# Cross-attention on one core: for two of four head groups GpSimd adds the two key halves of the probabilities, and the product with ones runs later on half as much

## What is computed

```python
def _L0_xattn_ref(q, v, k, Wq, bq, Wk, bk, Wv, bv, Wo, bo):
    NH = 16                       # heads of DK = 32
    qh = (q @ Wq.T + bq).reshape(b, s, NH, DK).transpose(0, 2, 1, 3)
    kh = (k @ Wk.T + bk).reshape(b, s, NH, DK).transpose(0, 2, 1, 3)
    vh = (v @ Wv.T + bv).reshape(b, s, NH, DK).transpose(0, 2, 1, 3)
    scores = einsum('bhqd,bhkd->bhqk', qh, kh) / sqrt(DK)
    probs = softmax(scores, axis=-1)
    ctx = einsum('bhqk,bhkd->bhqd', probs, vh)
    concat = ctx.transpose(0, 2, 1, 3).reshape(b, s, h)
    return concat @ Wo.T + bo
x = x + _L0_xattn_ref(_layernorm(x), ctx_1024, ctx_1024, ...)
```

## Time and profile before

| | us |
|---|---|
| median of 3 runs | 2575.8 (2575.73 to 2578.67) |
| the profiled execution, its own time | 2579.87 |
| its span in the profile | 2578.2 |
| TensorE (PE) busy | 2422.9 (94% of the span) |
| VectorE (DVE) busy | 1488.4 (58%) |
| ScalarE (ACT) busy | 1217.0 (47%) |
| GpSimd (POOL) busy | 651.0 (25%) |

### The profile page before, as it was taken

One profiled execution on the slowest core, in us unless ns is written; L12 is line 12 of the kernel. 1 busy time (PEld: TensorE's weight loads), 2 busy tenths in 40 slices (PEclk: granted clock), 3 DMA queues, 4 the chain that ended last, 5 costly groups with the idle time before them and its releaser, 6 DMA issues. The chain is left out here.

```text
span 2578.2 us, 47997 instructions
## 1 busy us (share of the span) xinstructions
PE 2422.9 (94%) x16982; PEld 2137.2 (83%) x16983; DVE 1488.4 (58%) x2585; ACT 1217.0 (47%) x1954; POOL 651.0 (25%) x1040
## 2 busy tenths in 40 slices
PE   7999999999997899999999983699999999999997
PEld 6999999999986788888888863488888888888896
DVE  6788888878873566666666655633343343334322
ACT  6655656656552444444444432334444353434342
POOL 3211111112114435454444511113030221303021
PEclk8999999999998899999999986799999999999999
DMA  4111111111126565656666522234152434424221
GB/s 133 39 40 50 39 38 56 35 44 48 39 65 179 146 199 154 191 165 187 177 180 184 157 86 86 65 110 108 67 133 75 110 82 126 103 73 113 89 59 20
DMA packets 237633, 261.01 MB, mean 101 GB/s; under 512 B 71112, under 2 KB 161224, under 8 KB 237360
## 3 DMA queue, kind: packets, MB, share of 16 engines
q1 hardware_dynamic: 196400, 237.48, 31.1%
q0 software_dynamic: 40960, 20.41, 4.5%
HBM read 182.47 MB, written 68.80 MB: 97 GB/s over the span
## 5 line engine op out<-in xcount | busy, mean ns | idle before, releaser
L2340 DVE TENSOR_TENSOR d_h_l<-d_hf,d_h_h 128x616 fp32r<-128x616 f32 x124 | 99.2, 800 | 391.0 <-ACT d_h_h L2137 391.0
L2037 PE MATMUL d_psH<-d_xgT_h,d_w_l 128*128 128x308 f32 x1024 | 314.7, 307 | 3.5 <-ACT d_hf L2189 2.1
L2189 ACT ACTIVATE d_hf<-d_psH,d_b1c 128x308 f32<-128x308 f32 x256 | 130.8, 518 | 385.8 <-PE d_psH L2039 385.8
L2038 PE MATMUL d_psH<-d_xgT_l,d_w_h 128*128 128x308 f32 x1024 | 311.5, 304 | 0.0
L2039 PE MATMUL d_psH<-d_xgT_h,d_w_h 128*128 128x308 f32 x1024 | 311.3, 304 | 0.0
L439 PE MATMUL a_psP<-s_xnT_h,s_w_l 128*128 128x256 f32 x1024 | 297.3, 290 | 5.8 <-ACT a_zs L691 2.7
L440 PE MATMUL a_psP<-s_xnT_l,s_w_h 128*128 128x256 f32 x1024 | 290.8, 284 | 0.0
L441 PE MATMUL a_psP<-s_xnT_h,s_w_h 128*128 128x256 f32 x1024 | 290.3, 284 | 0.0
L1999 POOL DMA_INDIRECT out_dram<-d_ob,d_to x40 | 103.7, 2592 | 686.0 <-ACT d_ob L2206 676.0
L2037 PE MATMUL d_psO<-d_w_h,d_h_l 128*123 128x512 f32 x620 | 244.2, 394 | 0.0
L2038 PE MATMUL d_psO<-d_w_l,d_h_h 128*123 128x512 f32 x620 | 244.0, 394 | 0.0
(11 more groups left out here) (399 smaller groups left out, 6103.0 us busy)
## 6 DMA issues: line engine op xcount, KB each, us to landing
d_w<-in_W_dram SPq DMA_DIRECT2D x64, 1024.0 KB, 6.4
b_qst<-qs_d SPq DMA_DIRECT2D x48, 512.0 KB, 6.7
b_kst<-ks_d SPq DMA_DIRECT2D x96, 256.0 KB, 4.0
s_raw<-in_x_dram SPq DMA_DIRECT2D x16, 512.0 KB, 3.6
s_xres<-in_x_dram SPq DMA_DIRECT2D x16, 512.0 KB, 3.6
x_d<-s_xres SPq DMA_DIRECT2D x16, 512.0 KB, 2.8
s_raw<-in_ctxT_dram SPq DMA_DIRECT2D x16, 512.0 KB, 9.6
s_xres<-x_d SPq DMA_DIRECT2D x16, 512.0 KB, 6.8
```

The source lines that it names most:

```text
L2037: pe.matmul(out, lo_w, hi_x, start=first, stop=False)
L2038: pe.matmul(out, hi_w, lo_x, start=False, stop=False)
L2189: act.activation(hf[:, m % 2, n * HALF:(n + 1) * HALF], psH[n][:, 0:HALF], ACT.Silu, bias=b1c[par][:, m:m + 1]).then_inc(silu_s, 1)
L2340: dve.tensor_tensor(out, a, b_, ALU.subtract).then_inc(done, 1)
```

## The change

For the groups j = 0 and 1 (`ADDED = 2`), `pv` does the product with V alone and raises a new semaphore `vp_mm`. GpSimd then adds the second key half of `PT` onto the first, in place (`pt_sum(j)`, one addition of 128 x 1024), and raises `pt_s`. TensorE does the product with ones later, on the added half alone (`sums(hb, j)`, 4 matmuls in place of 8, 8 instructions in place of 16): for group 0 behind turned(1,1), one K tile later, for group 1 behind K tile 7. `pv_mm` is now raised by `sums` for these two groups. Groups 2 and 3 stay as they are. In GpSimd's program pt_sum(0) stands between qk_parts(4) and max_parts(4), and pt_sum(1) between qk_parts(6) and max_parts(6); the `rsqrt` of sequence b-2 moves from behind max_parts(4) to ahead of pt_sum(0). ScalarE does exps(1,1) ahead of ctx_hi of group 0. VectorE does ctx_f of group 0 behind the third layer norm's `normalize` and row_max(2,1), and row_max(3,0) ahead of ctx_lo of group 0. In `experts_phase` two semaphores are merged into a third (`th_mm` and `mm_s` into `gr_mm`), with the waits raised to match; no instruction is added or moved there.

```diff
--- before.py
+++ after.py
@@ -1002,6 +1002,7 @@
         v_mm, v_cp = sem("v_mm"), sem("v_cp")
         s_mm, mx_s, mp_s, mt_mm, mr_s = (sem(n) for n in ("s_mm", "mx_s", "mp_s", "mt_mm", "mr_s"))
         st_mm, exp_s, pv_mm, cf_s, co_hi, co_lo = (sem(n) for n in ("st_mm", "exp_s", "pv_mm", "cf_s", "co_hi", "co_lo"))
+        vp_mm, pt_s = sem("vp_mm"), sem("pt_s")
         o_mm, x2_s, xb_s = sem("o_mm"), sem("x2_s"), sem("xb_s")
         r_tp, r_cp, r_mm, lg_s = sem("r_tp"), sem("r_cp"), sem("r_mm"), sem("lg_s")
 
@@ -1057,6 +1058,8 @@
         def second(b):
             return isinstance(b, int) and b == 1
 
+
+        ADDED = 2
         block = ctx.enter_context(nc.Block())
 
         @block.sync
@@ -1188,9 +1191,18 @@
                     g.tensor_tensor(mxp[:, j % 2, qt, KR + G:KX], mx[:, qt, :], f32(mxp[:, j % 2, qt, KR:KR + G]),
                                     ALU.subtract).then_inc(mp_s, 1)
 
+                def pt_sum(j):
+                    pool.wait_ge(vp_mm, ADDED * (b - 1) + j + 1)
+                    pool.sem_inc(passed_p, 1)
+                    g.tensor_tensor(PT[:, j % 2, :, 0, :], PT[:, j % 2, :, 0, :], PT[:, j % 2, :, 1, :], ALU.add).then_inc(pt_s, 1)
+
                 for i in range(U):
                     if cur:
                         qk_parts(i)
+                    if prev2 and i == 4:
+                        rsqrt(b - 2, ln3, ve3, rs3, rstd3)
+                    if prev and i in (4, 6):
+                        pt_sum(i // 2 - 2)
                     if prev:
                         max_parts(i)
                     if cur and i < KD and not first(b):
@@ -1204,8 +1216,6 @@
                             pool.wait_ge(p_ld, 96)
                         for t in range(TT):
                             g.tensor_tensor(xres[:, t, :], xres[:, t, :], bob[:], ALU.add).then_inc(xb_s, 1)
-                    if prev2 and i == 4:
-                        rsqrt(b - 2, ln3, ve3, rs3, rstd3)
                 if cur and not last(b) and not first(b):
                     rsqrt(b, ln, ve, rs, rstd)
                 if first(b):
@@ -1332,13 +1342,20 @@
                         wait(pe, x2_s, 2 * (b - 1))
                     if j == 2 and prev2:
                         pe.wait_ge(lg_s, b - 1)
-                    for half_, w in enumerate((V[v], None)):
+                    for half_, w in enumerate((V[v], None)[:1 if j < ADDED else 2]):
                         for kt in range(TT):
                             for h in range(G):
                                 c = slice((G * j + h) * DK, (G * j + h + 1) * DK)
                                 mm = pe.matmul(psV[h * DK:(h + 1) * DK, half_ * S:(half_ + 1) * S],
                                                ones[:] if w is None else w[:, kt, c], PT[:, j % 2, h, kt, :],
                                                start=kt == 0, stop=kt == TT - 1)
+                    mm.then_inc(vp_mm if j < ADDED else pv_mm, 1)
+
+                def sums(hb, j):
+
+                    pe.wait_ge(pt_s, ADDED * hb + j + 1)
+                    for h in range(G):
+                        mm = pe.matmul(psV[h * DK:(h + 1) * DK, S:2 * S], ones[:], PT[:, j % 2, h, 0, :], start=True, stop=True)
                     mm.then_inc(pv_mm, 1)
 
                 def out_proj(t):
@@ -1416,6 +1433,7 @@
                 if prev:
                     scores(2, 1)
                     turned(1, 1)
+                    sums(b - 1, 0)
 
                 if cur:
                     qk_tile(6)
@@ -1429,6 +1447,7 @@
                 if cur:
                     qk_tile(7)
                 if prev:
+                    sums(b - 1, 1)
                     turned(2, 0)
                     scores(3, 1)
 
@@ -1549,8 +1568,8 @@
                 if cur:
                     q_f(5)
                 if prev:
+                    exps(1, 1)
                     ctx_hi(b - 1, 0)
-                    exps(1, 1)
                 if prev2:
                     act.wait_ge(r_tp, b - 1)
                     copy(xn3T, psT[:], r_cp)
@@ -1674,15 +1693,15 @@
                         weights_lo(c)
                 if prev:
                     row_max(2, 0)
-                    ctx_f(b - 1, 0)
                 if prev2:
 
                     wait(dve, xn3_st, 16 * (b - 2))
                     normalize(b - 2, ln3, xres, mv3, rs3, rstd3, xn3)
                 if prev:
                     row_max(2, 1)
+                    ctx_f(b - 1, 0)
+                    row_max(3, 0)
                     ctx_lo(b - 1, 0)
-                    row_max(3, 0)
                 if more:
                     dve.wait_ge(xa_ld, 16 * b + 16)
                     for t in range(TT):
```

More of the change, by code:

```diff
@@ L1868, in experts_phase @@
         cn_s, th_s = csem("cn"), csem("th")
-        pre_s, mm_s = csem("pre"), csem("mm")
+        pre_s = csem("pre")
         key_s, cand_s, sign_s = csem("key"), csem("cand"), csem("sign")
-        gate_s, gt_mm, gr_mm, th_mm = csem("gate"), csem("gt_mm"), csem("gr_mm"), csem("th_mm")
+        gate_s, gt_mm, gr_mm = csem("gate"), csem("gt_mm"), csem("gr_mm")
         MADE = 12
@@ L2026, in _ @@
             pe.wait_ge(th_s, 1)
-            pe.matmul(psC, ones[:], digits[:].rearrange("p a e -> p (a e)"), start=True, stop=True).then_inc(th_mm, 1)
+            pe.matmul(psC, ones[:], digits[:].rearrange("p a e -> p (a e)"), start=True, stop=True).then_inc(gr_mm, 1)
             pe.wait_ge(made, MADE + 4)
@@ L2033, in _ @@
             pe.matmul(psA, ones_b[:], upto[:], start=False, stop=True)
-            pe.matmul(psC[:, 0:NE], ones_b[:], upto[:, 0, :, T - 1], start=True, stop=True).then_inc(mm_s, 1)
+            pe.matmul(psC[:, 0:NE], ones_b[:], upto[:, 0, :, T - 1], start=True, stop=True).then_inc(gr_mm, 1)
             def split_mm(out, hi_w, lo_w, hi_x, lo_x, first, last_):
@@ L2311, in _ @@
             dve.sem_inc(th_s, 1)
-            dve.wait_ge(th_mm, 1)
+            dve.wait_ge(gr_mm, ROUNDS + 1)
             did(dve.tensor_copy(hi_i[:], psC[:, 0:NE]))
@@ L2323, in _ @@
                                    both[:].rearrange("p a e t -> p (a e t)"), 0.0, ALU.mult, ALU.add).then_inc(pre_s, 1)
-            dve.wait_ge(mm_s, 1)
+            dve.wait_ge(gr_mm, ROUNDS + 2)
             did(dve.tensor_copy(cnt[:], psC[:, 0:NE]))
```

## The result

The changed kernel takes 2639.02 us (median of 4 runs, 2636.91 to 2644.08) against 2577.24 us of the kernel before on the same chip (2575.73 to 2580.93): a ratio of 1.0241, interval 1.0228 to 1.0254. It is 62 us slower; forecast were 50 us more and 2626 us. The profiled execution of it took 2639.2 us, its span is 2637.6 us.

A forecast was written before the change was run, and what follows sets the result against it. TensorE's program was taken as the bounding chain in attention, busy 392 of 400 us. Race 40, rest 2 and clock 8 gave 50 us on 2579.9, so 2630, or 2626 us for the median; range 2606 to 2644.

The forecast's parts named there:

- the race: After tile 6's take, TensorE needs one K tile, GpSimd split plus addition: 2.85 us in each of 14 bodies, 40 us.
- the clock in the full bodies: TensorE's clock drops behind new waits of 2.1 us: 6 of 14 bodies at 1.3 us, 8 us.
- The addition's price: GpSimd's addition of 128 x 1024, extrapolated from smaller two-input instructions: 2.36 us, bounds 2.0 to 3.1.
- The 0.28 us for contention: Extra time given to pt_sum(0) on GpSimd because VectorE's normalize runs beside it.
- Group 0: TensorE waits 0.9 us at sums(0), K tile 6 starts 0.75 us late, and this is absorbed before K tile 7.
- With 0.7 us of cover: ctx_f of group 0 ends at 1172.5, before pv of group 1 needs it at 1173.2, so costs nothing.
- K tile 7 starts at 1174.87 as before: Tile 6 is taken at 1174.34 as before, by store or copy; gains and losses ahead of it sum to 0.
- The rest: Body 1 1 us, body 15 perhaps 0.5, body 16 0.5; together 2 us; merged experts-phase semaphores cost nothing.
- The first: Rival: faster, sums never wait because pt_sum(1) ends before K tile 7; 9 us gained, 2567 us; chance 0.04.
- The second: Rival: no change, tile 6's take moves over a microsecond earlier and removed work pays the rest; 2571 to 2581; chance 0.04.
- The third: Rival: additions slow, 3.1 us each beside VectorE, 17 us on top, 2643 us; chance 0.12.

The follow-up runs named there:

- group 1 alone: Against the kernel before, only group 1 gets the addition and later sums; group 0 and all orders stay as before: 2640.05 us, ratio 1.0244.
- late sums: Group 1 alone with its addition ahead of qk_parts(6), sums behind scores(3,1) and the next context's load behind K's first half: 2585.82 us, ratio 1.0032.
- the late context: Next context's load issued behind K's first half in SyncE's program: kernel before 2574.02 us, ratio 0.9983; group 1 alone 2625.26 us, ratio 1.0197.

## Why the prediction was right, and where it was not

Direction, mechanism and range held; the forecast came 13 us low. Against the profiled execution's 59 us more (2639.2 against 2579.87), forecast as 50, the terms are: the race 40, forecast 40; tile 6 late 10, forecast 0; the clock in the full bodies 5, forecast 8; the ends 4, forecast 2. That the clock was put 3 us too high hid a part of the missing 10, and that is luck. Point by point:

- **The addition's price.** Taken 2.36 us, bounds 2.0 to 3.1; measured 2.37 in the mean (18 of them between 1000 and 1400). The step from 256 to 512 elements extends to 1024. The 0.28 us for contention was put on the wrong engine: pt_sum(0) took 2.38, and normalize paid 1.9 us.
- **Group 0.** A wait of 0.9 us was forecast; 0.50 came, for the most part because the addition was not slowed. "With 0.7 us of cover" failed: ctx_f started at 1197.58, 24.8 us into the body, instead of 24.1, since it queued behind the slowed normalize, and the product with V of group 1 waited 0.46 us. That made turn_rows' copy and tile 6 0.35 us late even where the store was in time.
- **"K tile 7 starts at 1174.87 as before ... is 0 in the sum."** This is the step that failed. Tile 6 was taken 0.79 us later in the mean, worth 10 us of the 51.8 in 13 periods, where the sum had 0. 0.35 of it is the row above; the rest is the store, whose landing I had pinned as a fixed time. It is not fixed: it moves by 1 us with the place of an instruction packet, and the change altered that place by taking 32 instructions out of each body.
- **Group 1, the race.** Forecast 2.85 us a body, a wait of 2.1; the wait measured 2.00 us, 2.72 to turned(2,0), 2.82 to the body's end, and moving the addition ahead of the split gave 29 us back in the whole change, the clock's share included, and 28 in group 1 alone, though there the clock fell more often. The term of 40 us stands.
- **The rest.** Taken 2 us; body 1 grew by 3.2, body 15 by 3.2, of which the race is 2.8, body 16 by 1.9, and what lies ahead of body 1 shrank by 1.2: 4 us. In body 1 the mean granted clock was 0.77 over 55.50 us, before 0.81 over 52.32. That is 25.5 us at the lower level against 19.9, an estimated 2.8 us at most of its 3.2; the forecast had no clock term for this body.
- **The clock.** Taken 6 of 14 bodies at 1.3 us, 8; measured 3 at 1.6 us, 5. In the windows above TensorE stood still for half of the 4 us from 1104, and in the 4 from 1109 the granted clock was 0.57, which is 3.4 us at the lower level.
- **The rivals.** The first was decided as said, by where the addition stands; even with it early, TensorE had no gain. The second needed tile 6 taken over a microsecond earlier; it was taken later. The third had the additions slow; they were not.

What was removed from TensorE was worth nothing on any of these kernels. With late sums, no wait for the addition, the normalizations undisturbed and the late context, the result (2585.82 us) is still above the kernel before with the late context alone (2574.02 us). Their two profiled executions, 17 us apart, divide it in part: the 13 periods from body 2 on are 9.3 us longer with the late sums, of which 5.3 are tile 6's later take, which goes with the packets, and 4.0 stand behind it, 0.3 a body, where the late sums are; body 1 is 1.1 longer, and how the rest falls is open. Open is also why the clock falls behind one wait of 2.0 us and not behind the next: the whole change had three such full bodies, group 1 alone with the late context seven, with the same wait in all.

## What to carry to other kernels

Before work moves from the fullest engine to an idle one, look at what the receiving program has ahead of the new step: here the addition stood behind an instruction released by the very event that also starts TensorE's last cover, and that alone set 40 of the 50 us forecast. Ask next what runs on VectorE beside a long GpSimd instruction, for here the one that started second stood still, and that was VectorE. And do not treat the landing of a transfer as a fixed time when an edit changes the number of instructions in a loop body; where a transfer is what a body waits for, moving its issue ahead of less urgent loads took 4 to 6 us off the kernel before (2574.02 against 2579.58 us), while no form of the edit itself gained anything.

## What the runs showed of the hardware that was not expected

- **VectorE beside GpSimd.** Two tensor_scalar of 128 x 512 took 2.98 us in place of 1.08 while GpSimd added 128 x 1024 in 2.38 us, against 2.35 when alone. The Trainium skill, GPSIMD Engine Reference, section 8 (Key points), says that GpSimd shares its SBUF interfaces with VectorE, with contention where VectorE's instruction is in a 2-port mode or has two SBUF inputs. The runs show the contention; in which mode normalize ran no row shows. The loss fell on VectorE nearly whole, whose instruction had started 0.14 us later; where normalize had started first, GpSimd's cast was the slower one.
- **Instruction packets.** A 16 KB packet, three to a body of 768 TensorE instructions, took about 1 us of one DMA engine, and the store queued behind the loads landed about 1 us later where it fell among them; by what way one packet holds the store up, no row shows. The Trainium skill, Runtime: NRT & Kernel Launch, section on instruction fetch mechanics, has blocks of 16 KiB for 256 instructions, which the trace bears out, and calls the cost of crossing one mostly hidden. For TensorE the waits shown here agree: none is for a packet. The transfers beside it did pay. Adding 16 instructions to a body made group 1 alone 10 us faster (2640.05 to 2630.3) and the kernel before 17 us slower (2578.16 to 2595.28), there for the most part through the store.
- **Semaphore increments on TensorE** cost some 0.10 us each (32 in 3.3 us); they hide only inside a standstill that is longer than they are.
- **The clock.** Only kernels in which TensorE stood still for some 2 us or more (1.9 to 3.3) once per body had it lowered in full bodies, and not in all of them; each time cost 1.4 to 1.6 us, and over 2 where it stayed low for twice as long.
